# Inner filters of batch 0 kept unscaled, with three sums a half, and the factor 0.5 moved to the copy out of the banks

## The chip, the core and the metric

The kernel runs on one core of a Trainium2 chip. The metric is the time of one launch on the device in microseconds (us). The engines are named as in the profile: PE (TensorE: matmul, with PEld for its weight loads), DVE (VectorE), ACT (ScalarE), POOL (GpSimd) and SP, whose queue (SPq) issues every DMA of this kernel.

## What is computed

A transformer layer over four sequences ("batches") of 512 tokens of width 1024. The part that matters here is the convolution ahead of the attention:

```
x = lax.conv_general_dilated(inputs, conv_w, window_strides=(1,), padding='SAME',
                             dimension_numbers=('NWC', 'WIO', 'NWC')) + conv_b
q, k, v = jnp.split(x, 3, axis=-1)
```

conv_w has three taps of 1024 x 768. Attention in blocks of 128 with 16 heads, an output projection, layer norms and a small mixture of low-rank experts follow. All of it is float32. A matmul is made of three passes over operands that are split into a high and a low part (`w_hi`, `w_lo`).

## The kernel before

**The convolution.** It makes two tokens at a time out of four products instead of six. The four filters of a channel block are tap 0 (j = 0), the two inner filters (tap 0 + tap 2 + tap 1) / 2 (j = 1) and (tap 0 + tap 2 - tap 1) / 2 (j = 2), and tap 2 (j = 3). There are six channel blocks c of 128, and I call the work on one block a turn: turns 0 to 5, in `C_ORDER`. Each filter comes in two halves of four row tiles, 128x512 numbers or 256 KB each, so a turn has 8 chunks, taken as (0,0) (0,1) (3,0) (3,1) (1,0) (1,1) (2,0) (2,1), named (filter, half). Turn 0 alone takes all four filters of half 0 and then those of half 1. For each chunk PE does 4 x 3 matmuls of 256 columns into the banks. After a turn, `conv_out` copies the two inner products out of the banks (ACT, `q_t`), POOL adds and subtracts them (`k_t`), and DVE's `conv_add` puts two results together (`prob`).

**Making the inner filters.** Batch 0 makes them and stores them in HBM (`summed_filters`); batches 1 to 3 load them. In batch 0 a half costs DVE five instructions (`sum_`): for j = 0 a copy of the raw chunk into `outer` (L1114), for j = 3 the addition of the other raw chunk (L1118) and a halving of tap 1 (L1120), and for j = 1 and j = 2 one SCALAR_TENSOR_TENSOR each (L1129), which is 0.5 outer + inner or 0.5 outer - inner. Every one of these four products of a turn is written to one of three buffers (`SUMS = 3`: two in `prob_t`, one in `prob`), from where ACT makes `w_hi` (L931), POOL or DVE makes `w_lo` (L1342, L1137), and SP stores it (L1433). The fourth of a turn, (2,1), writes the buffer of the first, (1,0), so it waits until the store of that has landed (`sum_kept`). I number these sum 1 to sum 4.

**The orders.** A planner (`Plan`) writes one list of stages, and every engine goes through its part of it in order. A chunk is split 5 chunks ahead of PE (`LEAD`), and summed one chunk ahead of its split (`SUM_LEAD`). Raw chunks have 6 slots; tap 1 of a turn has one place for both halves (`tap1`), loaded by `load_tap1` (L1426) right behind the load of chunk (0,0) of the same turn (L1403). So a turn's block of loads is (0,0), two halves of tap 1, (0,1), (3,0), (3,1): six DMAs of 256 KB. In `load_chunks` the block of a turn may be put in the list as soon as the j = 3, half 1 stage of the turn before is there, and SP waits at L1426 for `inner_full`, the halving of tap 1 in that turn.

Of the kernel before, what the change touches and what calls it, by code (L numbers as in the profile page):

```python
# [7 lines left out]
ALU = mybir.AluOpType  # L8
ACT = mybir.ActivationFunctionType
# [3 lines left out]
NB, L, D = 4, 512, 1024  # L13
# [5 lines left out]
C_ORDER = [4, 5, 0, 1, 2, 3]  # L19
# [3 lines left out]
L2 = L // 2  # L23
# [13 lines left out]
HALVES = KD // HALF  # L37
SLOTS = FILT * HALVES
ALL = NC * SLOTS
RAW_SLOTS, SPLIT_SLOTS = 6, 6  # L40
# [76 lines left out]
CHUNKS = chunk_names()  # L117
NUMBER = {name: k for k, name in enumerate(CHUNKS)}
# [7 lines left out]
LOADED = [k for k, name in enumerate(CHUNKS) if not is_summed(name)]  # L126
# [11 lines left out]
class Plan:  # L138
# [42 lines left out]
    def load_chunks(self):  # L181
        while self.loaded < len(CHUNKS):
            k = self.loaded
            name = CHUNKS[k]
            if not is_summed(name):
                n = LOADED.index(k)
                if n >= RAW_SLOTS and ("split", LOADED[n - RAW_SLOTS]) not in self.known:
                    break
                first = name[:2] == ("conv", 0) and name[3:] == (0, 0)
                if first and name[2] != C_ORDER[0]:  # L190
                    before = C_ORDER[C_ORDER.index(name[2]) - 1]
                    if ("sum", NUMBER["conv", 0, before, 3, HALVES - 1]) not in self.known:
                        break
                self.put("load", k)
                if first:
                    self.put("load_tap1", name[2])
            self.loaded += 1
# [287 lines left out]
def build(nc, x, conv_w, wq, wk, wv, wo, proj_w, biases, proj_b, aw, b_t, out):  # L485
    with ExitStack() as ctx:
# [3 lines left out]
        def sem(name):  # L490
            return ctx.enter_context(nc.semaphore(name))
# [21 lines left out]
        v = sb("v", [P, TB, H * DH])  # L513
# [14 lines left out]
        m12 = q_t[:, :].rearrange("p (j n) -> p j n", j=2)  # L528
        m12_sums = k_t[:, :].rearrange("p (j n) -> p j n", j=2)
        conv_out = prob[:, 0, :, :].rearrange("p t n -> p (t n)")  # L530
        tap1, outer, inner = v[:, 1, :], v[:, 2, :], v[:, 3, :]
        sums = [prob_t[:, 0, :], prob_t[:, 1, :], prob[:, 1, :, :].rearrange("p t n -> p (t n)")]
        lora_raw = [q_t, k_t]

# [9 lines left out]
        before = sb("before", [P, PR, E, E])  # L544
# [27 lines left out]
        def raw_of(k):  # L572
            if k in SUMMED:
                return sums[SUMMED.index(k) % SUMS]
            return raw_slots[LOADED.index(k) % RAW_SLOTS]
# [57 lines left out]
        filt_dve = Signal(sem("filt_dve"), at("filter_x"))  # L633
        f_low = Signal(sem("f_low"), at("x_lo"))
        filters = [CHUNKS[k][2:] + (k,) for (k,) in at("sum")]
        outer_kept = Signal(sem("outer_kept"), [(c, half) for c, j, half, k in filters if j == 0])
        outer_full = Signal(sem("outer_full"), [(c, half) for c, j, half, k in filters if j == 3])
        inner_full = Signal(sem("inner_full"), [(c, half) for c, j, half, k in filters if j == 3])
        sum_full = Signal(sem("sum_full"), [(k,) for c, j, half, k in filters if j in (1, 2)])
        split_low_dve = Signal(sem("split_low_dve"), [(k,) for (k,) in at("split") if low_on_dve(k)])  # L640
        even_out = Signal(sem("even_out"), at("conv_add"))
# [35 lines left out]
        raw_full, sum_kept, work_full, stored, tap1_full = Arrival(), Arrival(), Arrival(), Arrival(), Arrival()  # L677
# [27 lines left out]
        c_turn = lambda c: C_ORDER.index(c)  # L705
# [190 lines left out]
        def scalar_program(act):  # L896
            w = Waits(act)
# [40 lines left out]
            def conv_out_(b, turn):  # L938
                outer_bank, inner_bank, m2_bank, m3_bank = conv_places(b, turn)
                w.wait_ge(*conv_done(b, turn))  # L940
                if turn:
                    w.wait_ge(*m12_summed(b, turn - 1, 1))
                elif b:
                    w.wait_ge(*scored(b - 1, HP - 1, 1))
                else:
                    w.wait_ge(*lora_low(1))
                if m2_bank is inner_bank:
                    ins = act.activation(m12, inner_bank[:, :].rearrange("p (j n) -> p j n", j=2), ACT.Copy)  # L948
                else:
                    act.activation(m12[:, 0, :], inner_bank[:, 0:L2], ACT.Copy)  # L950
                    ins = act.activation(m12[:, 1, :], m2_bank[:, L2:L], ACT.Copy)
                ins.then_inc(*m12_out.now(b, turn))

            def conv_split(b, turn):
# [86 lines left out]
        def vector_program(dve):  # L1041
# [63 lines left out]
            def sum_(k):  # L1105
                _, b, c, j, half = CHUNKS[k]
                cols = slice(half * CHUNK, (half + 1) * CHUNK)
                src = raw_of(k)
                if j == 0:
                    w.wait_ge(*raw_full(k))  # L1110
                    earlier = [s for s in SUMMED if s < k]
                    if earlier:
                        w.wait_ge(*sum_full(earlier[-1]))
                    dve.tensor_copy(outer[:, cols], src[:, :]).then_inc(*outer_kept.now(c, half))  # L1114
                elif j == 3:
                    w.wait_ge(*raw_full(k))
                    w.wait_ge(*outer_kept(c, half))
                    dve.tensor_tensor(outer[:, cols], outer[:, cols], src[:, :], ALU.add).then_inc(*outer_full.now(c, half))  # L1118
                    w.wait_ge(*tap1_full(c, half))
                    dve.tensor_scalar(inner[:, cols], tap1[:, cols], 0.5, None, ALU.mult).then_inc(*inner_full.now(c, half))  # L1120
                else:
                    s = SUMMED.index(k)
                    if s >= SUMS:
                        w.wait_ge(*sum_kept(SUMMED[s - SUMS]))
                        w.wait_ge(*split_high(SUMMED[s - SUMS]))
                        w.wait_ge(*split_low(SUMMED[s - SUMS]))
                    w.wait_ge(*outer_full(c, half))
                    w.wait_ge(*inner_full(c, half))
                    dve.scalar_tensor_tensor(out=src, in0=outer[:, cols], scalar=0.5, in1=inner[:, cols],  # L1129
                                             op0=ALU.mult, op1=ALU.add if j == 1 else ALU.subtract).then_inc(*sum_full.now(k))  # L1130

            def split(k):
                if low_on_dve(k):
# [244 lines left out]
        def sync_program(sp):  # L1378
# [9 lines left out]
            def load(k):  # L1388
                name = CHUNKS[k]
                n = LOADED.index(k)  # L1390
                slot, full = raw_slots[n % RAW_SLOTS], s_raw[n % RAW_SLOTS]
                if n >= RAW_SLOTS:
                    earlier = LOADED[n - RAW_SLOTS]
                    w.wait_ge(*split_high(earlier))
                    w.wait_ge(*split_low(earlier))
                    if CHUNKS[earlier][:2] == ("conv", 0):
                        _, _, c, j, half = CHUNKS[earlier]
                        w.wait_ge(*(outer_full if j else outer_kept)(c, half))
                by_tile = slot[:, :].rearrange("p (k n) -> p k n", k=HALF)
                if name[0] == "conv":  # L1400
                    _, b, c, j, half = name
                    if j == 0:
                        sp.dma_start(by_tile, tap_half(0, c, half)).then_inc(full, 16)  # L1403
                    elif j == 3:
                        sp.dma_start(by_tile, tap_half(2, c, half)).then_inc(full, 16)
                    else:
                        if b == 1:
                            w.wait_ge(*sum_kept(NUMBER["conv", 0, c, j, half]))
                        sp.dma_start(slot[:, :], summed[c, j - 1, half]).then_inc(full, 16)
                elif name[0] == "v":  # L1410
                    _, b, half, kt = name
                    sp.dma_start(slot[:, :], wv[kt * P:(kt + 1) * P, half * 512:(half + 1) * 512]).then_inc(full, 16)
                elif name[0] == "proj":
                    _, b, t0, half, kt = name
                    sp.dma_start(slot[:, :], proj_w[kt * P:(kt + 1) * P, half * 512:(half + 1) * 512]).then_inc(full, 16)
                elif name[0] == "wo":
                    sp.dma_start(slot[:, 0:KW * P], wo[name[2] * P:(name[2] + 1) * P, :]).then_inc(full, 16)
                else:
                    for j, weights in enumerate((wq, wk)):
                        sp.dma_start(by_tile[:, j * KW:(j + 1) * KW, :], columns_of(weights, name[2] * P, P)).then_inc(full, 16)  # L1420

            def load_tap1(c):
                if c != C_ORDER[0]:
                    w.wait_ge(*inner_full(C_ORDER[c_turn(c) - 1], HALVES - 1))
                for half in range(HALVES):
                    sp.dma_start(tap1[:, half * CHUNK:(half + 1) * CHUNK].rearrange("p (k n) -> p k n", k=HALF),  # L1426
                                 tap_half(1, c, half)).then_inc(s_tap1[half], 16)
# [78 lines left out]
```

## Time and profile before

| | us |
|---|---|
| median of 3 runs | 950.44 |
| lowest and highest of them | 947.37, 952.57 |
| the profiled execution | 947.76 |
| its span, first to last instruction | 946.0 |
| PE busy | 776.5 (82%) |
| DVE busy | 688.2 (73%) |
| POOL busy | 526.1 (56%) |
| ACT busy | 494.1 (52%) |

The span is cut into four batches of some 230 us, and the change touches the instructions of batch 0 up to about 135 us. Outside that, only the copy into `q_t` differs. Since the engines run in fixed orders and wait for each other by semaphores, what matters is which wait ends last in that stretch; the busy shares above are means over stages with different limits. Starts are counted from the span's start.

### The profile page before, as it was taken

How to read it: one execution, taken by the hardware profiler on the slowest of the kernel's cores; microseconds unless marked ns; L12 is line 12 of the kernel's file. 1: busy time of each engine (PE TensorE's matmuls, PEld its weight loads, DVE VectorE, ACT ScalarE, POOL GpSimd, SP SyncE). 2: the span in 40 equal slices, each digit the busy share in tenths (PEclk: the TensorE clock that was granted, in tenths of full speed). 3: DMA queues.
4: the chain of work that ended last, by engine and by line, in shares of the span. 5: the costliest groups of instructions: out<-in, count | busy, mean ns of one | idle time of the engine just before them, and what ended most of it. 6: DMA issues, size and time to landing. Idle time of an engine off the chain costs nothing.

```text
span 946.0 us, 15442 instructions
## 1 busy us (share of the span) xinstructions
PE 776.5 (82%) x5136; PEld 687.6 (73%) x5136; DVE 688.2 (73%) x1796; ACT 494.1 (52%) x1156; POOL 526.1 (56%) x450
## 2 busy tenths in 40 slices
PE   2587788999949697999968887999986968997573
PEld 1487786888949685788968776788886967876472
DVE  6988777895887665987696675798597673555856
ACT  3443346875436345676536445777436445565332
POOL 2555574667673573676773564677783456444211
PEclk9889999999979897999988987999997979999856
DMA  7254662113724262212733345111743433113002
GB/s 212 74 157 129 209 208 76 40 57 98 248 68 146 80 226 85 57 45 81 247 109 106 118 149 164 45 52 51 236 143 90 125 119 125 49 53 123 1 0 89
DMA packets 108414, 106.15 MB, mean 112 GB/s; under 512 B 7600, under 2 KB 83376, under 8 KB 108336
## 3 DMA queue, kind: packets, MB, share of 16 engines
q1 hardware_dynamic: 108336, 105.18, 35.4%
q8 instruction: 41, 0.67, 0.3%
q14 instruction: 37, 0.30, 0.1%
HBM read 90.47 MB, written 14.68 MB: 111 GB/s over the span
## 4 chain that ended last, share of the span: by engine, by line
DVE 39%; PE 36%; ACT 9%; issue 9%; DMA 5%; POOL 1%; SPq 0%; DVEq 0%; ACTq 0%
PE bank L733 9%; PE bank L734 8%; PE bank L735 8%; ACT prob L981 5%; PE bank L867 3%; DVE newton L1067 3%; DVE prob_t L1200 3%; DVE filt L1097 2%; PE bank L810 2%; DVE newton L1068 2%; DVE ln_r L1069 2%; DVE ln_r L1065 2%; PE bank L829 2%; DVE prob L1184 2%; DMA work<-x 2%
## 5 line engine op out<-in xcount | busy, mean ns | idle before, releaser
L1342 POOL TENSOR_TENSOR w_lo<-raw,w_hi 128x512 fp32r<-128x512 f32 (+1 forms) x217 | 271.5, 1265 | 142.7 <-ACT w_hi L931 141.0
L733 PE MATMUL bank<-f_hi,w_hi 128*128 128x256 f32 x768 | 232.0, 302 | 40.2 <-POOL w_lo L1342 19.7
L734 PE MATMUL bank<-f_lo,w_hi 128*128 128x256 f32 x768 | 225.3, 293 | 0.0
L735 PE MATMUL bank<-f_hi,w_lo 128*128 128x256 f32 x768 | 224.8, 293 | 0.0
L931 ACT ACTIVATE w_hi<-raw 128x512 fp32r<-128x512 f32 (+1 forms) x280 | 162.0, 600 | 70.4 <-PE bank L735 59.3
L733 PEld LDWEIGHTS bank<-f_hi,w_hi 128*128 128x128 f32 x768 | 156.0, 203 | 47.2 <-ACT w_hi L931 19.1
L734 PEld LDWEIGHTS bank<-f_lo,w_hi 128*128 128x128 f32 x768 | 155.9, 203 | 0.8
L735 PEld LDWEIGHTS bank<-f_hi,w_lo 128*128 128x128 f32 x768 | 155.5, 202 | 0.0
L1353 POOL TENSOR_TENSOR prob<-prob,rtotal 128x512 f32<-128x512 f32 x64 | 84.4, 1331 | 123.4 <-DVE rtotal L1192 123.4
L981 ACT ACTIVATE prob<-prob,ntop 128x128 f32<-128x128 f32 x256 | 99.3, 390 | 36.5 <-DVE ntop L1188 36.5
L1137 DVE TENSOR_TENSOR w_lo<-raw,w_hi 128x512 fp32r<-128x512 f32 x63 | 55.9, 895 | 16.8 <-ACT w_hi L931 16.8
L733 PE MATMUL bank<-c_hi,w_hi 128*128 128x512 f32 x128 | 57.3, 448 | 8.1 <-DVE prob L1162 6.2
L810 PE MATMUL bank<-k_t,q_t 64*128 64x128 f32 x512 | 55.9, 289 | 8.3 <-DVE k_t L1176 8.2
L1184 DVE CUSTOM_DVE_ANT_0 prob<-bank,mask 128x128 f32<-128x128 f32 x256 | 58.4, 281 | 3.6 <-PE bank L810 3.5
L810 PEld LDWEIGHTS bank<-k_t,q_t 64*128 64x128 f32 x512 | 49.9, 191 | 14.9 <-issue 14.9
L860 PE MATMUL bank<-ident,v 128*128 128x128 f32 x128 | 23.0, 340 | 42.2 <-ACT v L902 42.2
L1368 POOL TENSOR_TENSOR work<-work,v 128x1024 f32<-128x1024 f32 x14 | 35.1, 2530 | 39.9 <-ACT v L902 39.7
L924 ACT ACTIVATE f_hi<-filt 128x1024 fp32r<-128x1024 f32 x28 | 29.6, 1058 | 51.1 <-POOL filt L1335 48.4
L1349 POOL TENSOR_TENSOR k_t<-q_t 128x256 f32<-128x256 f32 x48 | 38.0, 813 | 30.7 <-ACT q_t L948 26.0
L829 PE MATMUL bank<-prob_t,v 128*64 128x128 f32 x512 | 51.9, 279 | 2.9 <-DVE prob_t L1200 2.9
L1362 POOL TENSOR_TENSOR work<-work,v 128x1024 f32<-128x1024 f32 x14 | 33.8, 2433 | 34.1 <-ACT v L902 34.1
L734 PE MATMUL bank<-c_lo,w_hi 128*128 128x512 f32 x128 | 51.7, 404 | 0.0
(132 smaller groups left out, 1739.7 us busy)
## 6 DMA issues: line engine op xcount, KB each, us to landing
raw<-conv_w SPq DMA_DIRECT2D x96, 256.0 KB, 3.1
raw<-summed_filters SPq DMA_DIRECT2D x72, 256.0 KB, 2.8
work<-x SPq DMA_DIRECT2D x32, 512.0 KB, 5.6
raw<-proj_w SPq DMA_DIRECT2D x32, 256.0 KB, 2.9
out<-work SPq DMA_DIRECT2D x16, 512.0 KB, 3.8
summed_filters<-prob_t SPq DMA_DIRECT2D x16, 256.0 KB, 4.3
raw<-wv SPq DMA_DIRECT2D x16, 256.0 KB, 3.0
raw<-wq SPq DMA_DIRECT2D x32, 128.0 KB, 2.3
```

Of the source, the lines that this page charges most:

```text
L733: pe.matmul(dst, w_h, m_h, start=start, stop=False)
L734: pe.matmul(dst, w_h, m_l, start=False, stop=False)
L735: return pe.matmul(dst, w_l, m_h, start=False, stop=stop)
L810: ins = pe.matmul(score_banks[g][:, toks], q_t[rows, toks], k_t[rows, toks], start=True, stop=True)
L829: ins = pe.matmul(acc[g * DH:(g + 1) * DH, toks], v[:, t, head:head + DH], prob_t[:, g, toks], start=True, stop=True)
L931: act.activation(w_hi[k % SPLIT_SLOTS][:, 0:n], raw_of(k)[:, 0:n], ACT.Copy).then_inc(*split_high.now(k))
L981: ins = act.activation(prob[:, g, t, :], prob[:, g, t, :], ACT.Exp, bias=ntop[:, g, t:t + 1], scale=QK_SCALE, accum_out=total[:, g, t:t + 1])
L1137: dve.tensor_tensor(lo, raw_of(k)[:, 0:n], hi.bitcast(F32), ALU.subtract).then_inc(*split_low_dve.now(k))
L1184: ins = dve.tensor_tensor_reduce(prob[:, g, t, :], score_banks[g][:, t * P:(t + 1) * P], mask[:, :], 1.0, NEG_INF * 4, ALU.add, ALU.max, t ...
L1342: pool.tensor_tensor(lo, raw_of(k)[:, 0:n], hi.bitcast(F32), ALU.subtract).then_inc(*split_low_pool.now(k))
L1349: pool.tensor_tensor(m12_sums[:, i, :], m12[:, 0, :], m12[:, 1, :], op).then_inc(*m12_summed.now(b, turn, i))
L1353: pool.tensor_tensor(prob[:, g, :, :], prob[:, g, :, :], rtotal[:, g, :].rearrange("p (t o) -> p t o", o=1).broadcast_to([P, TB, P]), ALU. ...
```

## The change

It does five things.

- `sum_` does nothing for j = 0. For j = 3 it adds the two raw chunks in one TENSOR_TENSOR into `outer`. For j = 1 and 2 it adds or subtracts `tap1` itself, a TENSOR_TENSOR in place of the SCALAR_TENSOR_TENSOR. A half takes three DVE instructions in place of five (COPY, TENSOR_TENSOR, TENSOR_SCALAR and two SCALAR_TENSOR_TENSOR before).
- The inner filters, stored ones too, are twice as large, and ACT's copy into `q_t` has scale 0.5, in all batches.
- `tap1` is now read by all four sums, so its reload waits for `sum_full` of chunk (2,1) of the turn before, which is sum 4, no longer for `inner_full`.
- `load_chunks` puts a turn's block of loads in the list behind sum 4 of the turn before. Since a chunk of tap 0 now stays in its slot until it is added, its slot also waits for that sum.
- The signals `outer_kept` and `inner_full` go.

```
                 if n >= RAW_SLOTS and ("split", LOADED[n - RAW_SLOTS]) not in self.known:
                     break
+                if n >= RAW_SLOTS and CHUNKS[LOADED[n - RAW_SLOTS]][:2] == ("conv", 0):
+                    _, _, c, _, half = CHUNKS[LOADED[n - RAW_SLOTS]]
+                    if ("sum", NUMBER["conv", 0, c, 3, half]) not in self.known:
+                        break
...
-                    if ("sum", NUMBER["conv", 0, before, 3, HALVES - 1]) not in self.known:
+                    if ("sum", NUMBER["conv", 0, before, 2, HALVES - 1]) not in self.known:
...
-                    ins = act.activation(m12, inner_bank[:, :].rearrange("p (j n) -> p j n", j=2), ACT.Copy)
+                    ins = act.activation(m12, inner_bank[:, :].rearrange("p (j n) -> p j n", j=2), ACT.Copy, scale=0.5)
...
-                if j == 0:
+                if j == 3:
+                    first = NUMBER["conv", 0, c, 0, half]
+                    w.wait_ge(*raw_full(first))
                     w.wait_ge(*raw_full(k))
                     earlier = [s for s in SUMMED if s < k]
                     if earlier:
                         w.wait_ge(*sum_full(earlier[-1]))
-                    dve.tensor_copy(outer[:, cols], src[:, :]).then_inc(*outer_kept.now(c, half))
-                elif j == 3:
-                    w.wait_ge(*raw_full(k))
-                    w.wait_ge(*outer_kept(c, half))
-                    dve.tensor_tensor(outer[:, cols], outer[:, cols], src[:, :], ALU.add).then_inc(*outer_full.now(c, half))
-                    w.wait_ge(*tap1_full(c, half))
-                    dve.tensor_scalar(inner[:, cols], tap1[:, cols], 0.5, None, ALU.mult).then_inc(*inner_full.now(c, half))
-                else:
+                    dve.tensor_tensor(outer[:, cols], raw_of(first)[:, :], src[:, :], ALU.add).then_inc(*outer_full.now(c, half))
+                elif j in (1, 2):
...
                     w.wait_ge(*outer_full(c, half))
-                    w.wait_ge(*inner_full(c, half))
-                    dve.scalar_tensor_tensor(out=src, in0=outer[:, cols], scalar=0.5, in1=inner[:, cols],
-                                             op0=ALU.mult, op1=ALU.add if j == 1 else ALU.subtract).then_inc(*sum_full.now(k))
+                    w.wait_ge(*tap1_full(c, half))
+                    dve.tensor_tensor(src, outer[:, cols], tap1[:, cols], ALU.add if j == 1 else ALU.subtract).then_inc(*sum_full.now(k))
...
                     if CHUNKS[earlier][:2] == ("conv", 0):
                         _, _, c, j, half = CHUNKS[earlier]
-                        w.wait_ge(*(outer_full if j else outer_kept)(c, half))
+                        w.wait_ge(*outer_full(c, half))
...
                 if c != C_ORDER[0]:
-                    w.wait_ge(*inner_full(C_ORDER[c_turn(c) - 1], HALVES - 1))
+                    w.wait_ge(*sum_full(NUMBER["conv", 0, C_ORDER[c_turn(c) - 1], 2, HALVES - 1]))
```

The orders of PE, ACT and POOL stay as they are, instruction by instruction. DVE's and SP's change.

DVE, from sum 4 of turn 2 to the end of `conv_add` in turn 3. `prob<-v` and `prob_t<-v` are sums; `prob<-bank` and `prob<-k_t` are `conv_add`; `v<-...` makes `outer` (and, in the row with TENSOR_SCALAR, half of tap 1). Before:

```order
L1129 SCALAR_TENSOR_TENSOR prob<-v 128x512
L1168 TENSOR_TENSOR c_lo<-prob,c_hi 128x512
L1114 COPY v<-raw 128x512
L1137 TENSOR_TENSOR w_lo<-prob,w_hi 128x512
L1114 COPY v<-raw 128x512
L1118 TENSOR_TENSOR v<-v,raw 128x512
L1120 TENSOR_SCALAR v<-v 128x512
L1137 TENSOR_TENSOR w_lo<-raw,w_hi 128x512
L1118 TENSOR_TENSOR v<-v,raw 128x512
L1120 TENSOR_SCALAR v<-v 128x512
L1129 SCALAR_TENSOR_TENSOR prob_t<-v 128x512 x2
L1129 SCALAR_TENSOR_TENSOR prob<-v 128x512
```

Between sum 4 of one turn and sum 1 of the next, DVE has nine instructions.

The same place on DVE in the changed kernel:

```order
L1127 TENSOR_TENSOR prob<-v 128x512
L1165 TENSOR_TENSOR c_lo<-prob,c_hi 128x512
L1134 TENSOR_TENSOR w_lo<-prob,w_hi 128x512
L1118 TENSOR_TENSOR v<-raw 128x512
L1134 TENSOR_TENSOR w_lo<-raw,w_hi 128x512
L1118 TENSOR_TENSOR v<-raw 128x512
L1127 TENSOR_TENSOR prob_t<-v 128x512 x2
L1127 TENSOR_TENSOR prob<-v 128x512
L1134 TENSOR_TENSOR w_lo<-prob_t,w_hi 128x512
L1156 SCALAR_TENSOR_TENSOR prob<-bank,bias,k_t 128x256
L1159 SCALAR_TENSOR_TENSOR prob<-k_t,bias,bank 128x256
L1127 TENSOR_TENSOR prob_t<-v 128x512
```

Now five are left between them, and the order of the rest is the same.

SP's queue around turns 2 and 3. `raw<-conv_w` and `v<-conv_w` are a turn's block of loads (the second is tap 1), `summed_filters<-...` are the stores of sums 1 to 4. Before:

```order
L1433 DMA summed_filters<-prob_t 128x512
L1433 DMA summed_filters<-prob 128x512
L1433 DMA summed_filters<-prob_t 128x512 x2
L1403 DMA raw<-conv_w 128x4x128
L1426 DMA v<-conv_w 128x4x128 x2
L1403 DMA raw<-conv_w 128x4x128
L1405 DMA raw<-conv_w 128x4x128 x2
L1433 DMA summed_filters<-prob 128x512
L1433 DMA summed_filters<-prob_t 128x512 x2
L1433 DMA summed_filters<-prob 128x512
```

The first four stores are those of turn 1, the block is that of turn 3, and the stores of turn 2 stand behind it.

The same place on SP in the changed kernel:

```order
L1430 DMA summed_filters<-prob_t 128x512
L1430 DMA summed_filters<-prob 128x512
L1430 DMA summed_filters<-prob_t 128x512 x2
L1400 DMA raw<-conv_w 128x4x128
L1423 DMA v<-conv_w 128x4x128 x2
L1400 DMA raw<-conv_w 128x4x128
L1402 DMA raw<-conv_w 128x4x128 x2
L1430 DMA summed_filters<-prob 128x512
L1430 DMA summed_filters<-prob_t 128x512 x2
L1430 DMA summed_filters<-prob 128x512
L1400 DMA raw<-conv_w 128x4x128
```

The rows read alike, but the block between the stores of turn 1 and those of turn 2 is now that of turn 2 itself: every block has moved behind the four stores of one more turn.

## Rows read from the trace of the kernel before

**Rows 1.** Waits from 50 to 142 us: total, times, longest (us)

```profile
DVE prob_t L1129 <- DMA summed_filters<-prob_t: 9.6, 3, 3.9
...
PE bank L733 <- POOL w_lo L1342: 8.0, 4, 3.8
...
SPq L1426 <- DVE v L1120: 30.2, 4, 10.6
```

**Rows 2.** Timeline of SP, turn 3's stretch: start, duration (us), engine, line, operation

```profile
84.93 0.38 SPq L1403 DMA_DIRECT2D raw<-conv_w  x1
92.12 0.94 SPq L1426 DMA_DIRECT2D v<-conv_w  x2
...
95.67 0.98 SPq L1433 DMA_DIRECT2D summed_filters<-prob_t  x2
```

**Rows 3.** Timeline of DVE: sum 4 of turns 1 to 5

```profile
67.65 0.69 DVE L1129 SCALAR_TENSOR_TENSOR prob_t<-v 128x512 f32<-128x512 f32 x1 [3.85 <-DMA summed_filters<-prob_t]
...
83.78 0.69 DVE L1129 SCALAR_TENSOR_TENSOR prob<-v 128x512 f32<-128x512 f32 x1 [2.96 <-DMA summed_filters<-prob]
...
99.92 0.69 DVE L1129 SCALAR_TENSOR_TENSOR prob_t<-v 128x512 f32<-128x512 f32 x1 [2.49 <-DMA summed_filters<-prob_t]
...
116.88 0.69 DVE L1129 SCALAR_TENSOR_TENSOR prob_t<-v 128x512 f32<-128x512 f32 x1 [3.28 <-DMA summed_filters<-prob_t]
...
129.98 1.36 DVE L1129 SCALAR_TENSOR_TENSOR prob<-v 128x512 f32<-128x512 f32 x1
```

**Rows 4.** Timeline of DVE, turn 2: sum 1, then the second half of conv_add

```profile
75.32 0.68 DVE L1129 SCALAR_TENSOR_TENSOR prob<-v 128x512 f32<-128x512 f32 x1
...
80.34 0.48 DVE L1162 SCALAR_TENSOR_TENSOR prob<-k_t,bias,bank 128x256 f32<-128x256 f32 x1
```

**Rows 5.** Timeline of DVE in turns 0 and 1: removed instructions, conv_add of turn 0

```profile
19.00 0.83 DVE L1114 COPY v<-raw 128x512 f32<-128x512 f32 x1
...
21.42 0.83 DVE L1120 TENSOR_SCALAR v<-v 128x512 f32<-128x512 f32 x1
...
37.72 0.43 DVE L1114 COPY v<-raw 128x512 f32<-128x512 f32 x1
...
38.87 1.50 DVE L1120 TENSOR_SCALAR v<-v 128x512 f32<-128x512 f32 x1
...
51.25 0.41 DVE L1114 COPY v<-raw 128x512 f32<-128x512 f32 x1
...
63.32 0.48 DVE L1162 SCALAR_TENSOR_TENSOR prob<-k_t,bias,bank 128x256 f32<-128x256 f32 x1 [0.21 <-POOL k_t L1349]
```

**Rows 6.** Landing of the loads L1405 issued from 44.71 us, and of L1403 there

```profile
44.71 1.17 SPq L1405 DMA_DIRECT2D raw<-conv_w  x2
...
DMA to landing us min/median/max: 4.8/4.9/5.0
...
DMA to landing us min/median/max: 3.2/3.9/4.6
```

**Rows 7.** A store with nothing ahead of it: its issue and its landing

```profile
42.07 0.32 SPq L1433 DMA_DIRECT2D summed_filters<-prob  x1
...
DMA to landing us min/median/max: 2.1/2.1/2.1
```

**Rows 8.** L1118 up to 150 us (ns, min/median/max), and POOL's splits in turn 3

```profile
L1118 DVE TENSOR_TENSOR v<-v,raw x12: 677/1131/1779, 19.9 to 123.6; 128x512 f32<-128x512 f32 x12
...
85.79 4.48 POOL L1342 TENSOR_TENSOR w_lo<-raw,w_hi 128x512 fp32r<-128x512 f32 x3 [4.24 <-ACT w_hi L931]
```

**Rows 9.** Groups of DVE instructions, 0 to 250 us: count, busy us, mean ns

```profile
L1114 DVE COPY v<-raw 128x512 f32<-128x512 f32 x12 | 10.7, 908 | 0.1
...
L1120 DVE TENSOR_SCALAR v<-v 128x512 f32<-128x512 f32 x12 | 9.8, 813 | 0.0
```

**Rows 10.** ACT copies out of a bank: scale alone, and with a bias operand (ns)

```profile
L948 ACT ACTIVATE q_t<-bank x23: 574/597/608, 76.6 to 785.9; 128x512 f32<-128x512 f32 x23
...
L991 ACT ACTIVATE o_hi<-bank,bias x32: 665/668/690, 166.3 to 870.6; 128x512 fp32r<-128x512 f32 x32
```

More of the change, by code:

```diff
@@ L530, in build @@
         conv_out = prob[:, 0, :, :].rearrange("p t n -> p (t n)")
-        tap1, outer, inner = v[:, 1, :], v[:, 2, :], v[:, 3, :]
+        tap1, outer = v[:, 1, :], v[:, 2, :]
         sums = [prob_t[:, 0, :], prob_t[:, 1, :], prob[:, 1, :, :].rearrange("p t n -> p (t n)")]
@@ L635, in build @@
         filters = [CHUNKS[k][2:] + (k,) for (k,) in at("sum")]
-        outer_kept = Signal(sem("outer_kept"), [(c, half) for c, j, half, k in filters if j == 0])
         outer_full = Signal(sem("outer_full"), [(c, half) for c, j, half, k in filters if j == 3])
-        inner_full = Signal(sem("inner_full"), [(c, half) for c, j, half, k in filters if j == 3])
         sum_full = Signal(sem("sum_full"), [(k,) for c, j, half, k in filters if j in (1, 2)])
@@ L947, in conv_out_ @@
                 if m2_bank is inner_bank:
-                    ins = act.activation(m12, inner_bank[:, :].rearrange("p (j n) -> p j n", j=2), ACT.Copy)
+                    ins = act.activation(m12, inner_bank[:, :].rearrange("p (j n) -> p j n", j=2), ACT.Copy, scale=0.5)
                 else:
-                    act.activation(m12[:, 0, :], inner_bank[:, 0:L2], ACT.Copy)
-                    ins = act.activation(m12[:, 1, :], m2_bank[:, L2:L], ACT.Copy)
+                    act.activation(m12[:, 0, :], inner_bank[:, 0:L2], ACT.Copy, scale=0.5)
+                    ins = act.activation(m12[:, 1, :], m2_bank[:, L2:L], ACT.Copy, scale=0.5)
                 ins.then_inc(*m12_out.now(b, turn))
```

## The prediction, made before the changed kernel was run

> **What bounds the kernel now.** The change touches batch 0's convolution, so I looked first at the waits of that stretch, 50 to 142 us, and not at the busy shares of the whole. Two of them tell the story [rows 1]. DVE, which is busy most of this time, waits 9.6 us in three waits for `summed_filters` stores to land. SP waits 30.2 us in four waits at L1426, the load of tap 1, for DVE's halving L1120. PE is starved behind both, 8.0 us of it by POOL's `w_lo` alone.
>
> The timelines show how these hang together. Take turn 3. SP issues the first load of a block at 84.93 and then stands at L1426 until 92.12; the stores come only behind the whole block, at 95.67 [rows 2]. So the store of sum 1 is held up by loads that nobody needs yet, and sum 4, which writes the same buffer, waits for it: in turns 1 to 4 its row ends in a wait for that DMA of 2.5 to 3.9 us [rows 3]. Sum 4 is the beat of the stretch, since DVE takes nothing of the next turn before it. I measure a turn from the end of one sum 4 to the end of the next. The ends are 68.34, 84.47, 100.61, 117.57 and 131.34 (start plus duration, rows 3), so turns 2 to 5 take 16.1, 16.1, 17.0 and 13.8 us, together 63.0. Turn 5 is short because no block for a turn 6 stands ahead of its stores.
>
> **Part 1: fewer instructions while DVE is the bound (turn 0 and 1).** Up to `conv_add` of turn 0 the path goes through DVE's filters of x. Ahead of DVE's last `f_lo` stand five instructions that go: 0.83 + 0.83 + 0.43 + 1.50 + 0.41 = 4.0 us [rows 5]. PE's last chunks of turn 0 wait for that `f_lo`, and `conv_add` of turn 0 for them, so its end moves from 63.32 + 0.48 = 63.8 to 59.8. What is late next there is PE itself, which moves along. Sum 4 of turn 1 comes right behind. Before, it waited to 67.65 for its store; now the store of sum 1 has no block ahead of it, and a store alone lands in 2.1 us [rows 7], long before 59.8. Sum 4 of turn 1 ends at 59.8 + 0.7 = 60.5 in place of 68.3. **Part 1 gives 7.8 us.**
>
> **Part 2: the block of loads moves behind sum 4 (turns 2 to 5).** This is what the list of orders shows and the words of the change don't. Before, a block was issued one turn ahead of its use and its landing cost nothing; the cover was the sums, splits and matmuls of a whole turn. Now its issue starts at the end of sum 4, behind one store, and DVE's next addition needs it. A block in just this position, behind one store, can be read: the store issues at 42.07 [rows 7], the two loads L1405 begin at 44.71 and, half of 1.17 us later, at 45.3, and they land 5.0 and 4.8 us after issue [rows 6]. Counted from the end of sum 4, chunk (3,0) is there at 44.71 - 42.07 + 5.0 = 7.6 us and (3,1) at 8.0. I take these values, since they are of the same DMAs in the same order; the bounds are below.
>
> Then DVE makes `outer` twice, then sum 1. Each costs 0.68 us alone and up to 1.78 beside POOL [rows 8]; POOL's three splits of raw chunks take 4.48 / 3 = 1.5 us each [rows 8]. In the changed kernel they fall on just these instructions, as the chunks land late for both. Chunk (0,1), issued just ahead of the two, at about 2.0, lands at 2.0 + 4.6 = 6.6 [rows 6], ACT makes its `w_hi` by 7.3, so POOL is busy from 7.3 to 10.3 in turns 2 and 4. I let DVE go at one instruction per POOL instruction while that lasts: `outer` 7.7 to 9.1 and to 10.6, sum 1 to 11.3. In turns 3 and 5 a `w_lo` of a raw chunk stands between these on DVE: 12.3 in turn 3, where it is caught beside POOL, 12.0 in turn 5.
>
> From the end of sum 1 to the end of `conv_add` it is 80.82 - 76.00 = 4.8 us [rows 4], over ACT's `w_hi` and `q_t`, POOL's `k_t` and DVE. That chain is in the same order as before, and the stored sum 1 lands inside it (2.1 us). Sum 4 adds 0.7. So the turns take 16.8, 17.8, 16.8 and 17.5 us, together 68.9 in place of 63.0. **Part 2 costs 5.9 us.** Turn 5 carries most of it (13.8 to 17.5), since its sum 4 had no late store to gain from.
>
> PE is not the bound inside that: its waits for `w_lo` [rows 1] show that it is ahead of what it is fed, and the longer turns leave it more room.
>
> **Part 3: small things.** The two SCALAR_TENSOR_TENSOR per half become TENSOR_TENSOR: 0.68 us for either where nothing disturbs it [rows 4, 8], so 0. A copy at 0.5 on ACT: the same copy now takes 0.597 us, one with a bias operand 0.668 [rows 10]. A constant factor is nearest to the first row, so I take 0; the other end is 24 x 0.07 = 1.7 us later at most, and no row gives a reason for a gain. The 24 removed instructions are 10.7 + 9.8 = 20.5 us of DVE time [rows 9], of which only the 4.0 us of part 1 lie on the path; the rest would stand in the time in which DVE now waits for the block.
>
> **Sum.** -7.8 + 5.9 = -1.9 us. The profiled execution took 947.76 (span 946.0), which is 2.7 below the median of 950.44. So 945.9 for it, and **948.6** against the median.
>
> **Rivals.**
>
> - *DVE and POOL miss each other.* If POOL's splits don't fall on the additions, `outer` and sum 1 take 0.68 each from 7.7: sum 1 ends at 9.8 (10.4 with the extra `w_lo`), the turns take 15.3, 16.0, 15.3, 16.0, together 62.6, and the whole gives 7.8 + 0.4 = 8.2 us: 942.2. For it: L1118 does take 0.677 at its least [rows 8], and with fewer instructions between them the pattern may shift. Against: both wait for the same landings.
> - *The block lands sooner.* The bound from the rows is 3.9 us for a load of such a block (the median of L1403, rows 6) in place of 4.9: 1 us a turn, 4 us in all, 944.5. The Trainium skill, SBUF — State Buffer, section "The DMA setup-cost knee", fits a transfer as 2 us plus its bytes over 436 GB/s. As an estimate from that, the store and six loads (1.84 MB) would land within 6.2 us of the first issue, 1.8 us a turn sooner than the rows, and the sum would be 7.2 us lower, 941.3. The rows disagree with it both ways: 2.1 us for one 256 KB store, where it gives 2.6, and 8.0 for the block.
> - *Slower: the turn becomes the block plus a jammed DVE.* If every instruction behind the landing takes 1.78 us, sum 1 ends at 13.0 (14.8 in turns 3 and 5), the turns take 18.5 and 20.3, together 77.6: +14.6 - 7.8 = +6.8, 957.2. The point at which it tips is (63.0 + 7.8) / 4 = 17.7 us a turn, only half a microsecond above my mean of 17.2. A block that lands 0.5 us later already does it. Against the full price: POOL has only two or three raw splits to do there, and is done by 11.3.
> - *The blocks cost nothing.* If something hides the landing after all (PE far enough behind), the saved DVE time counts in full: -20.5 us, 929.9. The four waits of 30.2 us [rows 1] speak against slack in that queue.
>
> **How the numbers follow.** 0.50 for my sum, with a range of its own of 945 to 953; 0.27 for the first two rivals (942 to 945); 0.18 for the slower one, in full or half; 0.05 for the last. The range 940 to 956 leaves out the last rival, the full price of the slower one and a little of the rest. About 0.5%, 4.8 us, is what a measurement of this kernel can tell from no change. Faster by more than that (below 945.7): 0.30. Within it: 0.53. Slower (above 955.2): 0.17.
>
> **What would show it.** Sum 4 of turn 1 starts near 60 us without a wait for a DMA. The waits of SP at the tap 1 load for DVE are gone, as are those of sum 4 for its stores. In their place DVE's `outer` waits for `raw` or `v` loads in turns 2 to 5, some 5 to 6 us each, and ACT's `w_hi` of (0,0) and (0,1) too; PE's gap sits at the start of a turn instead of before its last chunk. Sum 4 of turn 5 ends near 129.5 where it ended at 131.3; from there all is shifted by the same 2 us. I am wrong in part 1 if `conv_add` of turn 0 moves by less than 4 us; in part 2 if turns 2 to 5 take clearly more or less than 69 us together; and in the cover if batches 1 to 3, which have no such sums, change by more than 1 us in length.

## The result

The changed kernel is slower by a little, where I had forecast a little faster.

| | us |
|---|---|
| before, median of 20 runs | 948.27 (944.59 to 952.57) |
| changed, median of 20 runs | 952.35 (948.75 to 956.23) |
| ratio | 1.0039, 95% interval 1.0027 to 1.0051 |
| forecast | 948.6 against 950.44, range 940 to 956 |
| span of the profiled executions | 946.0 before, 950.9 changed |

With 20 runs the median of before is 948.27; the 950.44 that I set out from was of three. So the forecast was a change of -1.9 us, and the measured one is +4.1.

Lines of the kernel after have other numbers: sums are L1127, `outer` is L1118, `w_lo` on DVE L1134, loads L1400, L1423 (tap 1) and L1402, stores L1430, POOL's `w_lo` L1339, ACT's `w_hi` L933 and its copy to `q_t` L950.

The waits of DVE from 50 to 142 us in the changed kernel (total, times, longest), to be read beside [rows 1]:

```profile
DVE v L1118 <- DMA raw<-conv_w: 16.5, 3, 7.2
DVE v L1118 <- issue: 7.2, 2, 6.4
```

The wait for stores is gone, as forecast. In its place stand 16.5 us for raw chunks in three waits, and one of 6.4 us, in turn 2, whose releaser the profile calls "issue" but which ends in the same way: the chunk lands at 72.7 and DVE starts at 72.8. The DVE timeline shows where: it is always the first `outer` of a turn, here in turns 3, 4 and 5. (In turn 5 DVE has before that stood 3.8 us for the `w_hi` of a chunk of the same block.)

```profile
90.24 0.69 DVE L1118 TENSOR_TENSOR v<-raw 128x512 f32<-128x512 f32 x1 [6.08 <-DMA raw<-conv_w]
...
108.76 3.39 DVE L1118 TENSOR_TENSOR v<-raw 128x512 f32<-128x512 f32 x2 [7.24 <-DMA raw<-conv_w]
...
126.77 3.35 DVE L1118 TENSOR_TENSOR v<-raw 128x512 f32<-128x512 f32 x2 [3.16 <-DMA raw<-conv_w]
```

SP's queue shows the cause, turn 3 again, beside [rows 2]:

```profile
82.74 0.32 SPq L1430 DMA_DIRECT2D summed_filters<-prob  x1
83.16 0.38 SPq L1400 DMA_DIRECT2D raw<-conv_w  x1
83.58 1.11 SPq L1423 DMA_DIRECT2D v<-conv_w  x2
84.80 0.46 SPq L1400 DMA_DIRECT2D raw<-conv_w  x1
85.36 0.99 SPq L1402 DMA_DIRECT2D raw<-conv_w  x2
94.92 0.94 SPq L1430 DMA_DIRECT2D summed_filters<-prob_t  x2
```

The block of turn 3 goes out right behind the store of turn 2's sum 4, and is done issuing 3.6 us after that sum; then SP has nothing to do for 8.6 us. Before, the same queue stood for 7 us *ahead* of tap 1. Sum 1 was then done about when tap 1 went out, and its store left only behind the rest of the block, 3 us later.

Sum 4 of turns 1 to 5, the beat of the stretch, beside [rows 3]:

```profile
62.67 1.38 DVE L1127 TENSOR_TENSOR prob_t<-v 128x512 f32<-128x512 f32 x1
...
81.71 1.00 DVE L1127 TENSOR_TENSOR prob<-v 128x512 f32<-128x512 f32 x1
...
99.53 1.38 DVE L1127 TENSOR_TENSOR prob_t<-v 128x512 f32<-128x512 f32 x1
...
117.56 1.01 DVE L1127 TENSOR_TENSOR prob_t<-v 128x512 f32<-128x512 f32 x1
...
135.52 1.36 DVE L1127 TENSOR_TENSOR prob<-v 128x512 f32<-128x512 f32 x1
```

None of them waits for a DMA any more. They end at 64.05, 82.71, 100.91, 118.57 and 136.88 (start plus duration). So turn 1 ends 4.3 us earlier than before (68.34) and turn 5 ends 5.5 us later (131.34). The turns 2 to 5 take 18.7, 18.2, 17.7 and 18.3 us, together 72.8 in place of 63.0. Most of the 5.5 us stays to the end: the last store of the output is issued at 942.6 us before and at 947.6 after, and the spans differ by 4.9.

### The profile page after: what moved, and what is told of

It is laid out like the page before. It is cut to its first block, busy times and chain, and to the rows that moved or that the text cites. A ratio compares the mean times of both kernels' runs of the same rounds, so it can differ in the third digit from the quotient of the medians.

```text
span 950.9 us, 15412 instructions
## 1 busy us (share of the span) xinstructions
PE 775.0 (81%) x5136; PEld 685.6 (72%) x5136; DVE 678.7 (71%) x1772; ACT 495.4 (52%) x1156; POOL 525.0 (55%) x450
## 4 chain that ended last, share of the span: by engine, by line
DVE 37%; PE 36%; ACT 9%; issue 9%; DMA 5%; SPq 3%; POOL 1%; DVEq 0%; ACTq 0%
PE bank L735 9%; PE bank L737 8%; PE bank L736 8%; ACT prob L983 5%; PE bank L869 3%; DVE newton L1069 3%; DVE prob_t L1197 3%; PE bank L812 3%; DMA raw<-conv_w 2%; DVE filt L1099 2%; PE bank L831 2%; DVE ln_r L1071 2%; DVE ln_r L1067 2%; DVE prob L1181 2%; DVE w_lo L1134 2%
## 5 line engine op out<-in xcount | busy, mean ns | idle before, releaser
L1339 POOL TENSOR_TENSOR w_lo<-raw,w_hi 128x512 fp32r<-128x512 f32 (+1 forms) x217 | 270.9, 1262 | 159.3 <-ACT w_hi L933 157.6
L933 ACT ACTIVATE w_hi<-raw 128x512 fp32r<-128x512 f32 (+1 forms) x280 | 163.4, 601 | 94.7 <-PE bank L737 57.2
L1134 DVE TENSOR_TENSOR w_lo<-raw,w_hi 128x512 fp32r<-128x512 f32 x63 | 55.2, 884 | 20.5 <-ACT w_hi L933 20.5
L862 PEld LDWEIGHTS bank<-ident,v 128*128 128x128 f32 x128 | 19.4, 181 | 44.1 <-ACT v L904 44.1
```

The lines of the kernel that those rows point to most:

```text
L862: ins = pe.transpose(dst[:, i * P:(i + 1) * P], y[t][:, kt * P:(kt + 1) * P], ident[:, :])
L933: act.activation(w_hi[k % SPLIT_SLOTS][:, 0:n], raw_of(k)[:, 0:n], ACT.Copy).then_inc(*split_high.now(k))
L1134: dve.tensor_tensor(lo, raw_of(k)[:, 0:n], hi.bitcast(F32), ALU.subtract).then_inc(*split_low_dve.now(k))
L1339: pool.tensor_tensor(lo, raw_of(k)[:, 0:n], hi.bitcast(F32), ALU.subtract).then_inc(*split_low_pool.now(k))
```

## The experiments

All times below are against runs of the kernel before on the same chip. For each I also read the ends of sum 4 in its profile, as above.

**e1: a second buffer for tap 1, loads where they were.** The new sums are kept. `inner` left a free place, which takes tap 1 of every other turn, so that the block can go out a turn ahead.

```
-        tap1, outer = v[:, 1, :], v[:, 2, :]
+        tap1s, outer = [v[:, 1, :], v[:, 3, :]], v[:, 2, :]
...
-                    if ("sum", NUMBER["conv", 0, before, 2, HALVES - 1]) not in self.known:
+                    if ("sum", NUMBER["conv", 0, before, 3, HALVES - 1]) not in self.known:
...
-                if c != C_ORDER[0]:
-                    w.wait_ge(*sum_full(NUMBER["conv", 0, C_ORDER[c_turn(c) - 1], 2, HALVES - 1]))
+                if c_turn(c) >= 2:
+                    w.wait_ge(*sum_full(NUMBER["conv", 0, C_ORDER[c_turn(c) - 2], 2, HALVES - 1]))
+                tap1 = tap1s[c_turn(c) % 2]
...
```

The lines left out give each of the two places its own semaphores and let the sums read the right one.

> The changed kernel with a second buffer for tap 1 (free since `inner` is gone), so that a turn's block of loads can stand where it stood before the change, one turn ahead of its use. All sums as in the changed kernel. Theory A (the block behind sum 4 is what costs, and the saved instructions are worth something): DVE no longer waits for raw chunks, turns 2 to 5 fall from 72.8 us together to 50 to 60 (PE's 96 matmuls or the store of sum 1 become the beat), sum 4 of turn 5 ends at 112 to 125 where it ends at 136.9 in the changed kernel and at 131.3 before; time 930 to 942. Rival B (the saved instructions are worth nothing because POOL paces DVE, and the place of the loads hardly matters): 946 to 952.

Measured: 931.02 against 947.68, ratio 0.982 (0.9789 to 0.9852). Turns 2 to 5 take 13.2, 13.2, 13.8 and 12.8 us, together 53.0, and sum 4 of turn 5 ends at 114.6. With the loads hidden DVE goes from turn 1 to turn 2 without a pause; its timeline there:

```profile
60.18 1.38 DVE L1127 TENSOR_TENSOR prob_t<-v 128x512 f32<-128x512 f32 x1
61.48 1.78 DVE L1165 TENSOR_TENSOR c_lo<-prob,c_hi 128x512 fp32r<-128x512 f32 x1
63.19 1.78 DVE L1134 TENSOR_TENSOR w_lo<-prob_t,w_hi 128x512 fp32r<-128x512 f32 x1
64.90 3.49 DVE L1118 TENSOR_TENSOR v<-raw 128x512 f32<-128x512 f32 x2
68.31 0.68 DVE L1127 TENSOR_TENSOR prob<-v 128x512 f32<-128x512 f32 x1
```

In the changed kernel the same `outer` begins 8.8 us behind sum 4; here it is 3.3 us. Rival B fell. Theory A held in its numbers, but what it named as the next beat, PE or the store of sum 1, is not what this timeline shows: DVE is busy throughout, and only the sum 4 of turn 4 waits for a store (1.4 us). The kernel is faster than the one before and than the changed one.

**e2: the old sums with the late block.** The two conditions on the loads are those of the changed kernel, the arithmetic that of the kernel before.

```
-                    if ("sum", NUMBER["conv", 0, before, 3, HALVES - 1]) not in self.known:
+                    if ("sum", NUMBER["conv", 0, before, 2, HALVES - 1]) not in self.known:
...
-                    w.wait_ge(*inner_full(C_ORDER[c_turn(c) - 1], HALVES - 1))
+                    w.wait_ge(*sum_full(NUMBER["conv", 0, C_ORDER[c_turn(c) - 1], 2, HALVES - 1]))
```

> The kernel before with its five instructions a half, but with the block of loads behind sum 4 and tap 1 waiting for sum 4, as in the changed kernel. Theory A: this has the whole cost and none of the gain. Two halvings and one copy more stand between the landing and sum 1, at 0.4 to 1.5 us each, so turns 2 to 5 take 76 to 82 us together, and the time is 955 to 963, above the changed kernel. Rival B: the place of the loads costs nothing, 948, as before.

Measured: 955.51, ratio 1.0078 (1.0055 to 1.0102). The place of the block alone costs 7.8 us. Turns 2 to 5 take 74.7 us together, under my range of 76 to 82 and only 1.8 us more than with the new sums. The copies stand ahead of the first `outer`, in the wait for its chunk: over the four turns it starts 30.8 us behind sum 4, where it is 32.3 in the changed kernel. The halvings add 2.7 us between there and sum 1, and the rest of the turns 0.6.

**e3: the old sums with two buffers for tap 1.** Tap 1 is halved in place; the waits are as in e1, and so are the lines left out.

```
...
-                    dve.tensor_scalar(inner[:, cols], tap1[:, cols], 0.5, None, ALU.mult).then_inc(*inner_full.now(c, half))
+                    dve.tensor_scalar(tap1[:, cols], tap1[:, cols], 0.5, None, ALU.mult).then_inc(*inner_full.now(c, half))
...
```

> The kernel before with its five instructions a half (tap 1 halved in place) and two buffers for tap 1, so that SP doesn't wait for the halving. With e1 it tells the worth of the two saved instructions when loads are early in both. Theory A: the loads are worth most of it, 932 to 944, and e1 is 2 to 8 us faster than this. If the saved instructions are worth nothing (rival B), e1 and this agree within 1 us.

Measured: 937.47, ratio 0.9889 (0.9867 to 0.9911). Turns 2 to 5: 56.9 us. Theory A held here too: e1 is 6.5 us faster than this. Together with e1, e2 and the two kernels there is now a table of both parts of the change (differences to before in us):

| | block early, two buffers | block as before | block behind sum 4 |
|---|---|---|---|
| old sums | -10.2 (e3) | 0 | +7.8 (e2) |
| new sums | -16.7 (e1) | | +4.1 (changed) |

The new sums are worth 6.5 us when the loads are hidden and some 3.7 us when they are late. The place of the block is worth 18 to 21 us between its ends. By the intervals each entry is known to 1 to 3 us, so the 6.5 and the 3.7 are not told apart, but the signs of both parts are clear. The change took a gain of about 4 and paid 8 for it. And the old sums with two buffers for tap 1 already gain 10 of e1's 17 us: most of e1's gain did not need the new sums.

**e5: tap 1 last in its block.** Late block and new sums as in the changed kernel, but (0,0), (0,1), (3,0), (3,1) are loaded first.

```
-                if first:
+                if name[:2] == ("conv", 0) and name[3:] == (3, HALVES - 1):
                     self.put("load_tap1", name[2])
```

> The changed kernel with the two loads of tap 1 moved from behind chunk (0,0) to the end of the block, since only sum 1 needs them. It tests the first term of a turn, the landing: chunks (0,1), (3,0) and (3,1) are issued 0.9 to 1.1 us sooner. Theory: DVE's `outer` starts that much sooner in each of turns 2 to 5 (6.5 to 7.5 us behind sum 4 in place of 7.5 to 8.8), turns 2 to 5 take 68 to 71 us together in place of 72.8, time 948 to 950. Rival (the transfers share their bandwidth and end together whatever their order): the same 952.

Measured: 941.81 against 946.23, ratio 0.9955 (0.9937 to 0.9973). The direction held, but I had expected 2 to 4 us off the changed kernel and it is 8.5 (-4.4 against +4.1, each against runs of the kernel before); turns 2 to 5 take 15.7, 16.3, 15.4 and 16.3, together 63.7 in place of 72.8. The rival (the transfers end together whatever their order) fell. For the size, here are the loads L1402 (chunks (3,0) and (3,1)) of turn 3, issue and landing, first in the changed kernel, then in e5:

```profile
85.36 0.99 SPq L1402 DMA_DIRECT2D raw<-conv_w  x2
...
DMA to landing us min/median/max: 4.8/4.9/5.0
```

```profile
79.02 0.99 SPq L1402 DMA_DIRECT2D raw<-conv_w  x2
...
DMA to landing us min/median/max: 4.0/4.2/4.5
```

They are issued 2.65 us behind sum 4 in the one and 1.54 in the other, and they also land 0.7 us sooner after issue, with two transfers of 256 KB fewer ahead of them. I had counted the first and forgotten the second. DVE's `outer` then starts 5.6 us behind sum 4 in turns 2 and 3 in place of 8.8 and 7.5, and 6.4 in turns 4 and 5 in place of 7.8 and 8.2.

Of the 9.1 us that the four turns save, 8.3 lie there, between sum 4 and the first `outer`. From that `outer` to the end of sum 1 it is 16.5 us in place of 17.3, and from there to sum 4 the same 23.2. So the gain is the landing almost alone. The issue explains 4.4 of the 8.3 us (1.1 a turn).

**e6: raw chunks of turns 2 to 5 split by DVE, POOL out of its way.** Changed kernel, eleven `w_lo` moved from POOL to DVE in `LOW_ON_DVE_FIRST` (16, 17, 18, 24, 26, 27, 32, 33, 34, 41, 43).

> The changed kernel with the low parts of all raw chunks of turns 2 to 5 made by DVE in place of POOL (11 of 16 move), so that POOL is idle while DVE makes `outer`. It tests the second term of a turn: DVE beside POOL. Theory: `outer` takes 0.7 us each in place of 1.7, and though three instructions more stand in between at 0.7, sum 1 ends about 11.1 us after sum 4 of the turn before, where it is 11.8 to 12.9; turns 2 to 5 take 67 to 71 us together in place of 72.8, time 946 to 951. Rival (the lateness is all in the landing): turns get longer by the added instructions, 74 to 78 us, time 953 to 957.

Measured: turns 2 to 5 take 68.4 us together, inside what the theory said, and sum 1 ends 10.6 to 11.1 us behind sum 4. Summary of L1118 (ns, min/median/max) over batch 0, changed kernel and e6:

```profile
L1118 DVE TENSOR_TENSOR v<-raw x12: 692/1729/1782, 20.1 to 128.4; 128x512 f32<-128x512 f32 x12
```

```profile
L1118 DVE TENSOR_TENSOR v<-raw x12: 683/693/1777, 20.2 to 124.8; 128x512 f32<-128x512 f32 x12
```

The median of the same instruction is 1.73 us with POOL at the same chunks and 0.69 without; in [rows 8] it was 1.13. DVE does eleven instructions more and still ends the stretch 4.0 us earlier (132.87 for 136.88). The time is 951.12, ratio 1.0033 (1.0017 to 1.0049), at the edge of the 946 to 951 that I expected and, by its interval, not told apart from the changed kernel's. In the profiled executions the 4 us are still there at the end (spans of 946.5 and 950.9), but that execution of e6 was 2.8 us faster than its median and had the highest mean granted clock of its eight (0.924, the others 0.912 to 0.922; 0.917 in the changed kernel's). Why the medians show no more than about 1 us of the 4 stays open.

**e4: the block behind sum 2.** e1 with the gate one step later, so that the first two stores leave ahead of it.

```
-                    if ("sum", NUMBER["conv", 0, before, 3, HALVES - 1]) not in self.known:
+                    if ("sum", NUMBER["conv", 0, before, 1, HALVES - 1]) not in self.known:
```

> e1 with a turn's block of loads put in the list behind sum 2 of the turn before, so that in most turns the stores of sums 1 and 2 leave before it. In e1 one turn's sum 4 still waited 1.4 us for a store to land, and the turns took 12.8 to 13.8 us. Theory: that last wait goes, and nothing comes in its place, since the block is still there half a turn ahead of its use: turns 2 to 5 together 50 to 53 us in place of 53.0, time 929 to 932, the same as e1 within what can be measured. Rival: loads half a turn later are late again for the splits, 934 or more.

Measured: 932.34 against 946.23, ratio 0.985 (0.9829 to 0.987), whose interval overlaps with that of e1. The last wait of sum 4 for a store went, but turns 2 to 5 take 55.3 us together in place of 53.0, over the 50 to 53 of the theory. What came in its place is the wait that e1 had removed; DVE's waits from 58 to 118 us in e4:

```profile
DVE v L1118 <- DMA raw<-conv_w: 7.0, 3, 3.2
```

In e1 there is none. The block half a turn later is late again for `outer` in turns 3 to 5, as the rival had it, though the time stays under its 934 us. It is no gain over e1.

**e7 and e8: turn 0 without POOL's low parts.** Changed kernel and kernel before, with POOL's `w_lo` of turn 0 cut to one column. POOL fills the `w_lo` buffers with zeros at the start, which takes it 2.8 us and is done by 3.6, and it still makes its part of the filters of x. These two kernels leave out low parts that the layer needs, and serve for this stretch alone.

```
...
-                    n = width_of(k)
+                    n = 1 if k < SLOTS else width_of(k)
```

> With e8 a test of why the removed instructions of turn 0 gave only 1.8 us where I had counted 4.0. Both leave out POOL's low parts in turn 0 but for one column (zeros stand in their place), the rest is the changed kernel here and the kernel before in e8. I read the stretch from DVE's first filter of x to the end of its last `f_lo` of batch 0, 33.1 us with the new sums and 34.9 with the old ones. Theory (POOL, or the wait beside it, takes what the removed instructions give back): with POOL out of the way the new sums are 3 to 4 us shorter than the old ones, something like 28 to 31 us here. Rival (another chain, over ACT, sets the pace): the difference stays at 1.8.

> The kernel before with POOL's low parts of turn 0 left out but for one column, as in e7. Theory: from DVE's first filter to the end of its last `f_lo` 31 to 34 us, 3 to 4 longer than e7; rival: 1.8 longer than e7.

Measured, from DVE's first filter of x to the end of its last `f_lo`:

| | old sums | new sums | difference |
|---|---|---|---|
| POOL as it is | 34.9 | 33.1 | 1.8 |
| POOL's low parts of turn 0 out | 30.4 (e8) | 28.0 (e7) | 2.4 |

Both numbers of the first row came back within 0.05 us in every other kernel of the study with the same sums and POOL as it is. e7 and e8 were run once each (947.37 us for e7, 945.12 for e8), and only this stretch is read from them. The difference grows when POOL does less, but to 2.4 and not to 3 or 4: neither my theory nor the rival's 1.8. The other part is in what I had counted as the cost of the removed instructions. The second halving of tap 1 took 1.50 us in [rows 5]; in e8, with POOL's two `w_lo` beside it cut to one column, the same instruction is

```profile
37.98 0.42 DVE L1121 TENSOR_SCALAR v<-v 128x512 f32<-128x512 f32 x1
```

so 1.1 of its 1.50 us were a wait beside POOL, and the five together are 2.9 us in e8, not 4.0. Take the halving away and the next instructions wait in its place. That is what the changed kernel shows there, where the two that follow took 1.57 and 1.10 us before:

```profile
38.91 1.70 DVE L1127 TENSOR_TENSOR prob<-v 128x512 f32<-128x512 f32 x1
40.53 1.75 DVE L1134 TENSOR_TENSOR w_lo<-prob_t,w_hi 128x512 fp32r<-128x512 f32 x1
```

The Trainium skill, SBUF — State Buffer, section "Who interferes with whom", says that DVE and GpSimd share a port pair as an exclusive lock, and that a DVE instruction with two SBUF inputs contends for it with a GpSimd one that reads SBUF. The trace agrees for such an instruction: a median of 0.69 against 1.73 us for L1118, in e6 and in the changed kernel.

## Why the prediction was wrong

The step that failed is the sizing of the two terms. Part 2, the block on the path, was counted at 5.9 us and measured at 9.8; part 1, the saved instructions, was counted at 7.8 and measured at 5.4. Either error alone takes the gain away: -7.8 + 9.8 = +2.0, and -5.4 + 5.9 = +0.5.

The account by the ends of sum 4 is complete. The changed kernel's first filter starts 1.1 us later (18.99 for 17.89), which belongs to the start of that execution and not to the change: in the eight kernels of the study it lies anywhere from 17.0 to 19.1. From there, +1.1 - 5.4 + 9.8 = +5.5 us, where I had -7.8 + 5.9 = -1.9.

*The picture was right.* The beat of sum 4, the store held up by the block, the block moved onto the path, the waits that go and those that come: each stands in the trace as described. So does part 3: the copy at 0.5 takes 597 ns in the middle, the same as without it,

```profile
L950 ACT ACTIVATE q_t<-bank x23: 574/597/607, 77.5 to 790.6; 128x512 f32<-128x512 f32 x23
```

and the sums take 675 and 677 ns at their least in the two forms. The loss is made in batch 0 and stays, to within what can be read: the lateness is 6.0 us at the last store of batch 0's output and 5.0 at the end. One of the batches 1 to 3 is 1.3 us shorter than before, over the 1 us that I had named as a sign of being wrong in the cover; but in the ten profiles of the study the lengths of batches 1 and 2 lie anywhere from 215 to 219.5 us, so that sign was finer than the trace.

*Step 1, part 1: 7.8 us counted, 5.4 measured.* Counted from the first filter, sum 4 of turn 1 ends at 45.1 us in place of 50.5. I had taken the durations of the five removed instructions, 4.0 us, as what the path gains. The last `f_lo` came 1.8 us earlier and the end of `conv_add` 2.1, under the 4 us that I had given as the sign of being wrong here. Durations that contain a wait beside POOL were added up as if they were the instructions' own. And I had overlooked that turn 1's block moves too, behind sum 4 of turn 0: DVE's `outer` of turn 1 waits 0.8 us for it, and in e1, with the same sums and the block early, sum 4 of turn 1 ends at 44.4 us in place of 45.1. The rest of the gap is that sum 4 was then not 0.7 but 1.38 us long, beside POOL as well, so that of the store's late landing 3.2 us were saved where I had counted 3.8.

*Step 2, part 2: 68.9 us counted, 72.8 measured.* In three terms, for four turns together:

| | counted | measured |
|---|---|---|
| sum 4 to the first `outer` (landing) | 30.8 | 32.3 |
| `outer`, `outer`, sum 1 | 16.1 | 17.3 |
| end of sum 1 to end of sum 4 | 22.0 | 23.2 |

Every term was too short by a twentieth or so, and all in the same direction. The landing was right to half a microsecond in turns 3 to 5 (7.5, 7.8, 8.2 against 7.7) and 1.1 us short in turn 2, where the two loads took 6.0 and 6.2 us after issue. (I had also read [rows 6] the wrong way round: in that block chunk (3,0) landed 4.8 us after its issue and (3,1) 5.0, so the rows give 7.4 and 8.2 us, not 7.6 and 8.0.) The DVE term was short because I gave an instruction beside POOL 1.5 us, the length of POOL's, where it takes 1.7. The last term again took sum 4 at 0.7 where it is 1.0 to 1.4.

*The balance.* I gave the tipping point as 17.7 us a turn, with my own mean at 17.2. The measured mean is 18.2. With part 1 at its measured 5.4 the tipping point is (63.0 + 5.4) / 4 = 17.1 us, below even my own mean. The slower rival named the mechanism, a jammed DVE behind the landing, and priced it at its worst, 77.6 us for the four turns; 3.9 of the 8.7 us from my 68.9 to there were gone. Two terms of 6 to 10 us with opposite signs, each known to no better than 2 us, don't settle a sign. A chance of 0.17 for "slower" by over 4.8 us may pass; that my central case stood on the other side of zero was the mistake. With ends of 0.68 and 1.78 us in hand I took 1.5 for `outer` beside POOL and 0.7 for sum 4. Measured, seven of the eight `outer` of turns 2 to 5 took 1.67 to 1.78 us, and sum 4 of turns 1 to 5 took 1.0 to 1.4.

## What to carry to other kernels

When an edit lets a buffer live longer, look at who reloads it and at everything in the queue behind that reload: here the two DVE instructions saved in each half were worth some 4 to 6.5 us, and the load that now waited for the last reader cost 8, until a second buffer, which the same edit had freed, turned the whole into a gain of 17. Try the buffer by itself as well: halving in place frees it without the new sums, and gave 10 of the 17. The durations of DVE's instructions in this trace hold their waits beside POOL; what the five gave back when they were removed (1.8 us, 2.4 with less of POOL) was nearer to their undisturbed durations (2.9) than to the measured ones (4.0). And when loads are on the path, put those that are needed first at the head: in e5 they were issued 1.1 us sooner and landed 0.7 us sooner after that.

## What was unexpected in the hardware

The gain from the order of six equal transfers. Moving two of them to the end of a block took 8.3 us off the wait for the landing in four turns, almost twice the 4.4 that the issue time alone gives. One transfer of 256 KB with nothing ahead lands in 2.1 us, and one behind five or six others 4.8 to 6.2 us after its own issue. In turn 3 of the changed kernel the six loads are issued 0.55 us apart and land 0.9 us apart, so each one that stands ahead adds to the time from issue to landing.
